# A Mamba-style mixer's clipped states: corrections on stretches of 256 steps with a lead of 32, in place of rows of 1024

## The reference

```python
def step(h, x_t):
    h = jnp.clip(h * A[None] + x_t[:, :, None] * Bm[None], -10.0, 10.0)
    y = jnp.einsum('bid,id->bi', h, C)
    return (h, y)
...
A = -jnp.clip(jnp.exp(A_log), -10.0, -0.01)
out_f = _ssm_scan(x_ssm, A, B_mat, C_mat, reverse=False)
out_b = _ssm_scan(x_ssm, A, B_mat, C_mat, reverse=True)
out = (out_f + out_b) * 0.5 * jax.nn.silu(gate)
return jnp.einsum('bli,di->bld', out, out_proj_w)
```

## Time and profile before

| | us |
|---|---|
| median of 3 runs | 3723.31 |
| lowest, highest | 3721.92, 3731.75 |
| the profiled execution's own time | 3721.55 |
| its span | 3719.6 |

### The profile page before, as it was taken

The page is one execution under the profiler, slowest core; times in us unless marked ns, Lnnn a source line. Parts: engine busy times, 40 slices in busy tenths (PEclk is TensorE's granted clock), DMA queues, the critical chain, the costliest instruction groups (busy, mean ns, idle before and its releaser), DMA issues. The chain is left out here.

```text
span 3719.6 us, 31897 instructions
## 1 busy us (share of the span) xinstructions
PE 2784.2 (75%) x10138; PEld 1394.3 (37%) x10146; DVE 2052.8 (55%) x3662; ACT 1359.4 (37%) x1980; POOL 897.8 (24%) x608
## 2 busy tenths in 40 slices
PE   2006898999999889999777867937888888287317
PEld 1003444555555534444344442423222222055303
DVE  7997432222222465655544476126766666587687
ACT  1003433111111256666434311415666666243003
POOL 0003565000000000000122402133777777200004
PEclk6558999999999999999778879979999999599558
DMA  2001121000000275455100020120000000100001
GB/s 50 0 0 46 46 62 47 0 0 0 0 0 0 49 139 146 138 147 139 32 1 1 1 71 20 57 58 30 1 1 2 7 1 0 31 1 1 2 0 29
DMA packets 107447, 125.99 MB, mean 34 GB/s; under 512 B 22283, under 2 KB 60300, under 8 KB 107052
## 3 DMA queue, kind: packets, MB, share of 16 engines
q1 hardware_dynamic: 105260, 120.13, 12.4%
q0 software_dynamic: 2048, 4.20, 0.4%
HBM read 108.55 MB, written 14.16 MB: 33 GB/s over the span
## 5 line engine op out<-in xcount | busy, mean ns | idle before, releaser
L2349 PE MATMUL dots_x<-all_xt,delta_wE 128*128 128x512 f32 x768 | 369.0, 614 | 70.1 <-DVE dots_g L2465 68.6
L2332 POOL TENSOR_TENSOR dots_pr<-dots_g 128x1536 f32<-128x1536 f32 (+2 forms) x98 | 296.1, 3043 | 143.6 <-DVE dots_g L2465 119.1
L1012 DVE SCALAR_TENSOR_TENSOR attn_sim<-attn_sc,attn_mask 128x512 f32<-128x512 f32 (+3 forms) x256 | 125.8, 491 | 316.9 <-PE attn_sc L938 313.8
L938 PE MATMUL attn_sc<-attn_q,attn_xb 128*128 128x512 f32 (+3 forms) x768 | 295.0, 486 | 0.0
L949 PE MATMUL attn_op<-attn_sim,attn_v 128*128 128x512 f32 (+3 forms) x768 | 295.0, 486 | 0.0
L2462 DVE TENSOR_TENSOR dots_m<-dots_x,dots_sg 128x512 f32<-128x512 f32 x256 | 170.3, 685 | 213.0 <-ACT dots_sg L2384 124.7
L1298 DVE TENSOR_TENSOR grp_h<-grp_sq,grp_cb 128x512 f32<-128x512 f32 x256 | 176.5, 692 | 192.1 <-ACT grp_sq L1186 171.8
L1126 PE MATMUL grp_po<-grp_h,grp_down 128*128 128x512 f32 x512 | 266.4, 602 | 6.0 <-DVE grp_h L1298 6.0
L1118 PE MATMUL grp_ph<-all_xt,grp_up 128*128 128x512 f32 x512 | 263.9, 598 | 0.5 <-ACT grp_sg L1202 0.5
L2349 PEld LDWEIGHTS dots_x<-all_xt,delta_wE 128*128 128x128 f32 x768 | 134.6, 190 | 304.6 <-issue 160.8
L1180 ACT ACTIVATE grp_r<-grp_ph 128x512 f32<-128x512 f32 x272 | 162.4, 597 | 185.5 <-PE grp_ph L1118 183.8
(11 more groups left out here) (614 smaller groups left out, 4961.9 us busy)
## 6 DMA issues: line engine op xcount, KB each, us to landing
grp_cb<-grp_combine SPq DMA_DIRECT2D x512, 128.0 KB, 3.2
mix_cb<-top_weights SPq DMA_DIRECT2D x64, 256.0 KB, 3.2
cap_xs<-cap_zero SPq DMA_DIRECT2D x7, 320.0 KB, 4.4
experts_xe<-cap_xs SPq DMA_DIRECT2D x7, 320.0 KB, 3.4
all_x<-in_L_attn_x_dram SPq DMA_DIRECT2D x4, 512.0 KB, 5.2
cap_w<-in_L_ffn_W_dram SPq DMA_DIRECT2D x1, 2048.0 KB
cap_ys<-experts_yo SPq DMA_DIRECT2D x8, 256.0 KB, 2.3
delta_h<-all_xn SPq DMA_DIRECT2D x1, 2048.0 KB
```

The lines of the kernel that those rows point to most:

```text
L938: nc.tensor.matmul(sc[k % SC][:, 0:w], xb[:, m * P:(m + 1) * P], q[:, par, n0:n0 + w], start=True, stop=True).then_inc(s_mm, 1)
L2332: nc.gpsimd.tensor_tensor(slot[w % SLOTS][:, at:at + n], a_, b_, ALU.mult).then_inc(pool_ready, 1)
L2349: nc.tensor.matmul(bank(n, sh)[:], wE[:, 1 - k % 2, a, sh], XTj[:, k // 2, par::2], start=True, stop=True).then_inc(u_mm, 1)
```

## The change

`LEAD, CHUNK` = 32, 256. Each row of 1024 steps is cut into `NCHUNK` = 4 stretches; a row and a stretch make a cell, 16 per batch (`NCELL`). The scan of S still covers the whole row. S now has 32 zero columns ahead of each row, so that each stretch can be read with the 32 steps before it.

- `reaches` keeps one largest value per stretch; `reach` grows from 64 to 256 columns, and with it what POOL reduces, the flags and the masks (16).
- `corrections` walks over 4 rows and in each over 4 stretches, and tests the mask of each cell.
- `correct` works on a window of 288 steps: the scan starts at zero, 32 steps before the stretch, and only the last 256 go into G.
- The semaphore `fix` becomes one per batch and counts 3 per state in place of 4, because the first `tensor_scalar` signals nothing any more.
- `d0`, `d1` and `q` shrink to the window, and the incoming weights are put in `y` instead of `q`.

The cut diff:

```diff
+    LEAD, CHUNK = 32, 256
+    NCHUNK = SEQ // CHUNK
+    NCELL = NSEG * NCHUNK
+    WINDOW, ROW = LEAD + CHUNK, LEAD + SEQ
...
-        d0 = s.sb("d0", [P, SEQ, 2])
+        d0 = s.sb("d0", [P, WINDOW, 2])
...
-        reach = s.sb("reach", [P, NSEG, DS])
+        reach = s.sb("reach", [P, NSEG, NCHUNK, DS])
...
-                def correct(b, k, d):
-
+                def correct(b, k, c_, d):
                     n = k * DS + d
-                    done = (b * (NSEG * DS) + n) * 4
-                    sk = S[:, bass.ds(k, 1), :].rearrange("p a t -> p (a t)")
-                    gk = G[:, bass.ds(k, 1), :].rearrange("p a t -> p (a t)")
+                    done = ((k * NCHUNK + c_) * DS + d) * 3
+                    sk = S_flat[:, bass.ds(k * ROW + c_ * CHUNK, WINDOW)]
+                    gk = G_flat[:, bass.ds((k * NCHUNK + c_) * CHUNK, CHUNK)]
...
-                    ts(d1[:, :, 0], sk, -1.0, L, ALU.mult, ALU.add).then_inc(fix, 1)
-                    ts(d1[:, :, 1], sk, L, None, ALU.add).then_inc(fix, 1)
-                    dve.wait_ge(fix, done + 2)
+                    ts(d1[:, :, 0], sk, -1.0, L, ALU.mult, ALU.add)
+                    ts(d1[:, :, 1], sk, L, None, ALU.add).then_inc(fix[b], 1)
+                    dve.wait_ge(fix[b], done + 1)
...
-                    stt(gk, q[:, :, 1], w, gk, ALU.mult, ALU.add).then_inc(fix, 1)
+                    stt(gk, q[:, LEAD:, 1], w, gk, ALU.mult, ALU.add).then_inc(fix[b], 1)
...
-                    c.link(redu(mx[:], S[:], AX.X, ALU.max, apply_absolute_value=True))
+                    c.link(redu(mx[:], S[:, :, LEAD:].rearrange("p k (c t) -> p k c t", t=CHUNK), AX.X, ALU.max, apply_absolute_value=True))
...
                     with dve.Fori(0, NSEG) as k:
-                        mask = dve.value_load(masks[0:1, bass.ds(k, 1)], min_val=0, max_val=2 ** DS - 1)
...
+                        with dve.Fori(0, NCHUNK) as c_:
+                            mask = dve.value_load(masks[0:1, bass.ds(k * NCHUNK + c_, 1)], min_val=0, max_val=2 ** DS - 1)
+                            for quad in range(DS // QUAD):
+                                with dve.If((mask & (((1 << QUAD) - 1) << (quad * QUAD))) > 0):
+                                    for d in range(quad * QUAD, (quad + 1) * QUAD):
+                                        with dve.If((mask & (1 << d)) > 0):
+                                            correct(b, k, c_, d)
+                                        with dve.Else():
+                                            dve.sem_inc(fix[b], 3)
+
+                                    dve.sem_inc(apart, 1)
+                                with dve.Else():
+                                    dve.sem_inc(fix[b], 3 * QUAD)
```

More of the change, by code:

```diff
@@ L266, in mixer_and_top2 @@
         limS, nCBS = (s.sb(n, [P, NSEG, DS]) for n in ("limS", "nCBS"))
-        d0 = s.sb("d0", [P, SEQ, 2])
[L268 to L271, removed]
-        xs, gate, y = (s.sb(n, [P, CT, SEQ]) for n in ("xs", "gate", "y"))
-        S, G = (s.sb(n, [P, NSEG, SEQ]) for n in ("S", "G"))
-        mx = s.sb("mx", [P, NSEG, 1])
-        reach = s.sb("reach", [P, NSEG, DS])
[L276 to L280, removed]
+        d0 = s.sb("d0", [P, WINDOW, 2])
+        d1 = s.sb("d1", [P, WINDOW, 2])
+        q = s.sb("q", [P, WINDOW, 2])
+        xs, gate, y = (s.sb(n, [P, CT, SEQ]) for n in ("xs", "gate", "y"))
+        wi = y[:, 0, 0:2 * CT * C].rearrange("p (k c) -> p k c", k=2 * CT)
+        wo = y[:, 1, 0:DI]
+        S = s.sb("S", [P, NSEG, ROW])
+        G = s.sb("G", [P, NSEG, SEQ])
+        S_flat, G_flat = S[:].rearrange("p k t -> p (k t)"), G[:].rearrange("p k t -> p (k t)")
+        mx = s.sb("mx", [P, NSEG, NCHUNK])
+        reach = s.sb("reach", [P, NSEG, NCHUNK, DS])
+        most = s.sb("most", [P, NCELL * DS])
+        bit = s.sb("bit", [1, NCELL, DS])
+        flags = s.sb("flags", [1, NCELL, DS])
+        mask_f = s.sb("mask_f", [1, NCELL])
+        masks = s.sb("masks", [1, NCELL], mybir.dt.int32)
         gw = s.sb("gw", [P, E])
@@ L304, in mixer_and_top2 @@
             "w_in", "c_in", "w_mm", "w_copied", "exp_ready", "pj_mm", "pj_used", "scanned", "y_ready"))
-        reach_ready, most_ready, out_mm, x_added, ch, fix, apart = (s.sem(n) for n in (
-            "reach_ready", "most_ready", "out_mm", "x_added", "vector_chain", "fix", "apart"))
+        reach_ready, most_ready, out_mm, x_added, ch, apart = (s.sem(n) for n in (
+            "reach_ready", "most_ready", "out_mm", "x_added", "vector_chain", "apart"))
+        fix = [s.sem(f"fix{b}") for b in range(BATCH)]
         gates_in, w1_in, w2_in, stats_done, var_ready, std_ready, xn_ready = (s.sem(n) for n in (
@@ L635, in largest @@
                     pool.sem_inc(apart, 1)
-                    nc.gpsimd.partition_all_reduce(most[:], reach[:].rearrange("p s d -> p (s d)"), P, bass.bass_isa.ReduceOp.max).then_inc(most_ready, 1)
+                    nc.gpsimd.partition_all_reduce(most[:], reach[:].rearrange("p s c d -> p (s c d)"), P, bass.bass_isa.ReduceOp.max).then_inc(most_ready, 1)
                 largest(0)
@@ L719, in corrections @@
                     with dve.Fori(0, NSEG) as k:
-                        mask = dve.value_load(masks[0:1, bass.ds(k, 1)], min_val=0, max_val=2 ** DS - 1)
[L721 to L731, removed]
+                        with dve.Fori(0, NCHUNK) as c_:
[10 more added lines that the diff above has]
+                                    dve.sem_inc(fix[b], 3 * QUAD)
                 def gated(b):
                     dve.wait_ge(pj_used, 8 * b + 8)
-                    dve.wait_ge(fix, (b + 1) * NSEG * DS * 4)
+                    dve.wait_ge(fix[b], NCELL * DS * 3)
                     for ct in range(CT):
@@ L788, in _ @@
                 c.link(ts(decay[:], al[:, 0, 0:1], -1.0, None, ALU.mult))
[L789 removed]
+                c.link(ts(d0[:, :, 0], al[:, 0, 0:1].to_broadcast([P, WINDOW]), 1.0, None, ALU.mult))
                 c.link(nc.vector.memset(d0[:, :, 1], -1.0))
+                c.link(nc.vector.memset(S[:, :, 0:LEAD], 0.0))
                 c.link(stt(nCB[:], Cm[:], -0.5, B[:], ALU.mult, ALU.mult))
```

11 lines of the change are left out of this document (6 added, 5 removed).

## The result

| | before | after |
|---|---|---|
| median, us | 3730.12 | 3716.92 |
| lowest, highest | 3721.92, 3734.82 | 3714.71, 3726.22 |
| runs | 12 | 12 |
| ratio, 95% interval | | 0.9972 (0.9962 to 0.9982) |
| the profiled execution's own time, span | 3721.55, 3719.6 | 3726.22, 3724.2 |

By the ratio the change saves 0.28%, some 10 us (7 to 14); the two medians alone differ by 13.2. In another set of runs (e5, nine of them) the ratio was 0.9977 (0.9968 to 0.9987). The forecast of 3704 was a gain of 19 us, a ratio of 0.995, which lies outside the interval. So the sign is right and about half of the gain is missing; by the bound of 0.3% used in the prediction, the change falls just within "no change".

What follows compares the result with a forecast made beforehand. It took PE's wait for the first gated product, set by batch 0's walk on DVE, as the bound: -79.9 + 54.6 + 5.4 + 0.8 = -19.1 us, 3702.4 for the profiled execution, stated as 3704; range 3687 to 3723.

Steps and rivals of the forecast that it cites:

- Part 2: DVE's walk: an empty cell costs 2.63 us, twelve more per batch 31.6, loop 1.5; batch 0 saves 79.9 in all.
- Part 3: Batches 1 to 3: the same 12 added cells make PE wait 31.5, 9.3 and 13.8 us for y, sum 54.6.
- the low clock: PE's clock drops during each new wait, so the small matmuls after it run slower: 1.8 us each, 5.4 together.
- Part 1: Batch 0 on DVE: 28 shorter corrections of 2.13 us each, 59.6 together, plus sequencer gaps of 42.3 us.
- The give-back: Batches 1 to 3: with POOL idle, slow y instructions take 1.22 in place of 2.18 us, returning 1.9, 2.8 and 2.8.
- The small terms: Reach products and flags on the path 0.8 us, wider flags and masks 0.4 per batch, the POOL reduction 0 (0 to 19).
- Each pass stalls: Rival: the walk's loop body misses the instruction buffer every pass, 1.8 us extra per cell, 115 on top, 3819; chance 0.07.
- Dear reduction: Rival: POOL's reduction over 256 columns costs 8 us in batch 0, up to 5.5 in batches 2 and 3; chance 0.12.
- Hidden walk: Rival: the added walk in batches 1 to 3 is hidden, giving 3704 - 60 = 3644 us; chance 0.03.
- More cells hit: Rival: more cells need corrections than worked out; four more with 28 corrections would cost 102 us; chance 0.02.
- wrong if: Signs against the forecast: mask loads over 2.9 apart, DVE waiting for POOL before flags, or no PE wait in batches 2 and 3.
- The first rival: Each pass stalls: all 64 cells count once cover is used up; beyond 0.3 us extra per cell the kernel is slower; chance 0.07.

Runs made afterwards that it cites:

- e5: The changed kernel measured once more, unaltered, as a comparison: 3739.8 us, ratio 0.9977 to the kernel before.
- e6: The changed kernel with its walk as one flat loop over 16 cells, one counter in place of two nested loops: 3732.8 us, ratio 0.9957 to the kernel before.
- e7: The changed kernel with stretches of 128 in place of 256, so 32 cells per batch: 3906.7 us, ratio 1.0418 to the kernel before.
- e1: The changed kernel with one test per row that skips rows without a set bit: 3683.8 us, ratio 0.9816 to the kernel before.
- e4: The kernel before, plus one test per batch that skips the walk where no row has a bit: 3756.5 against 3753 us, ratio 1.0007.
- e9: The changed kernel testing only one cell per row, where this input's hits lie: 3625.2 us, ratio 0.9722 to the kernel before.

## Why the prediction was half right

The bound was read rightly: PE waits for the first y, and the walk of batch 0 is its price. The mechanism came as described: 28 corrections, idle time called "issue" before every one of them, three new waits at the output product, of about 31, 9 and 14 us forecast and 31.45, 12.25 and 17.16 measured. The sum was forecast as -19.1 us for the stage and came out as -5.5:

| from, to | forecast | measured |
|---|---|---|
| start to output product 0 | -79.1 | -74.3 |
| product 0 to 1 | +31.5 | +33.0 |
| product 1 to 2 | +9.3 + 1.8 | +13.7 |
| product 2 to 3 | +13.8 + 1.8 | +19.7 |
| product 3 to the end | +1.8 | +2.4 |

(Measured: the starts in the earlier trace rows and in the profile after, for example 282.93 - 193.10 - (324.24 - 267.39) = 33.0.)

- **The step that failed is Part 2, the price of an empty cell**, which Part 3 multiplies. It was taken from rows of the old loop (2.63 us, plus 1.5 per batch for the loop). The new loop pays 116 ns more for the address ahead of the load and 22 more behind it, some 0.15 us a cell, on all 16 cells of a batch, not on the 12 new ones only, and 0.31 at each new row. Against the old walk, from the first to the last mask load, batch 1's is 42.24 - 8.08 = 34.2 us longer and those of batches 2 and 3 are 35.2 longer, where 33.1 was taken: 1.1 + 2.1 + 2.1 = 5.3 of the 13.6 missing. In batch 0 the twelve empty cells and the row steps took 34.5, 1.4 more. Together 6.7 us; the rest of the 13.6 is corrections and gaps in batch 0 (3.1), the low clock (1.5) and 2.3 of small pieces that I can't assign one by one. The diff showed the address, `k * NCHUNK + c_` in the mask's load; the list of built steps did not, since it has one ISA step ahead of the load before and after. I priced a dearer address in the corrections (0.1 each) and not in the cells. e6 undid the second counter and the stage fell by 12.9 us, to 18.6 below the kernel before. Of the 12.9, shorter walks are 11.1 (1.8 to the first y, then 3.1, 3.2 and 3.0 from first to last mask load, all against e5). That it ends so near the forecast is partly luck: in e6 the terms of the table are -76.3, +29.3, +11.4, +15.2 and +1.8, so that 2.8 too little in batch 0 stands against 2.2 too much forecast for batch 1.
- **Part 1 was right to 3 us of 105.** A correction took 2.21 us for 2.13 forecast (the tensor_scalars 0.28 and 0.40 to the next start for 0.25 and 0.37, the product 0.17 behind the scan), 2.2 us over 28. The scan took exactly the 1.36 worked out. The gaps come to 66.8 - 2.2 of idle, plus 27 times 0.49 of product, less 34.5 of empty cells, which is 43.2 for 42.3. The whole walk, from 45.52 (the end of the cast before it) to 188.04, was 142.5 for 137.9, and the first gated product came at 188.04, not near 182.
- **The cost of the low clock was a term of its own size, not 1.8 each.** The 32 products after a new wait took 5.17, 6.74 and 6.17 us where they had taken 3.73 to 3.75: 6.9 us for 5.4. Three stretches of the changed kernel (the last 9.5 us of the wait in batch 1, the output products of batch 1, those of batch 2) show the clock, the last but two of the numbers: 0.50, its lower level (1.2 of 2.4 GHz), while PE waits, 0.73 over the products that follow and 0.55 over those of batch 2:

```profile
273.40:282.90 9.50, 0.00 (x0) 0.00 (x0) 4.90 (x4) 0.00 (x0) 0.00 (x0) 0.50 0.00 1
282.90:288.10 5.20, 5.17 (x33) 5.17 (x34) 4.58 (x2) 0.00 (x0) 0.00 (x0) 0.73 0.00 0
385.40:392.20 6.80, 6.75 (x33) 6.75 (x34) 4.58 (x2) 0.00 (x0) 0.00 (x0) 0.55 0.00 0
```

- **What was hidden, and what came back.** The give-back was right: with POOL idle all four instructions of y took 1.22 or 1.23 us in each of batches 1 to 3. The small terms were not quite: 0.4 us more for flags and masks was 0.4, the reduction 0.5 more, and the walk of batch 0 began 1.0 us later for up to 0.8 forecast.
- **The rivals.** Each pass stalls: refuted. Behind the first cell of a walk, cells of one row lay 2.72 to 2.87 us apart with 16 cells and with 32 (e7; once 3.07), and the stall of 2 us came once per walk at most, in batches 2 and 3 and not in batch 1. (The "13 later passes" that the prediction counts against this rival are 7 in its rows.) The Trainium skill (Runtime: NRT & Kernel Launch, section on instruction fetch mechanics) ties a stall to a branch target outside the two blocks held. By that rule a body that did not fit would stall in every pass, and none did behind the first cell. That the stall is a fetch, no run here shows, nor why batch 1 has none. Dear reduction: refuted for this size, 1.06 to 1.23 us. Hidden walk: refuted by e1. More cells hit: no, the scans are 28.
- **The chances.** The "wrong if" bound on mask loads, over 2.9 us apart, was nearly reached (2.81, 2.89 and 2.88 on average in batches 1, 2 and 3). The first rival said that every extra microsecond per cell costs 64, and I did not apply this to the forecast's own 2.63. An uncertainty of 0.2 us a cell is 13 us, as much as the whole forecast's spread to one side, and with it "within 0.3%" would have had far more than 0.13.

The stage's 5.5 us and the 9 to 10 us measured for the whole program do not agree to the last microseconds. The profiled execution is one of twelve with a spread of 11.5 us. The traces show how much the later stages, whose code is the same, move by themselves: they took 3100.7 us in the profile before and 3110.8 after. Over half of these 10.1 us lies in one stretch of a later layer, from the first row of its `out_` tiles to the first row of the `sink_` tiles behind it: 258.9 us before and 265.2 after. It took 266.8 in e4, which is the kernel before with one test, and 258.9 in e9, which is the changed one with fewer cells, so it does not follow the change. The stage with the `attn_` tiles took 653 us in some profiled executions of either kernel and 656 in others. So the span of one execution says little about a difference of 10 us, and why the whole program gained more than the stage stays open.

## What to carry to other kernels

When a change cuts work into more pieces, price the piece that does nothing first: its cost times all pieces of all passes, not only the new ones, and ask for each whether its cover is used up. Price a sequencer's loop by the instructions of the new loop, address arithmetic included; here a second loop counter cost 12.9 us of the stage, over twice what the change left as a gain in it. And test from the outside in, batch, then cell, then bit: with that, one counter and a lead of 8, the same change was worth 96 us instead of 10.

## What the runs showed that was not expected

- A row address from one loop counter took 63 ns in DVE's sequencer, from two counters 179 (e5, e6); one load of a mask took 0.30 us in the median whatever the kernel, and a cell whose mask is zero still cost 1.50 (flat) to 1.63 us (two levels) with a single test.
- The reduction over the partitions on POOL took 0.54 us for 64 columns, 1.08 for 256 and 1.80 for 512 (medians): about 0.36 us plus 2.8 ns a column, far from in proportion.
- The scan on DVE took 825 ns at 320 columns, 1258 at 528, 1358 at 576, 2425 at 1088 and 4425 at 2048: 2.08 ns a column and 0.16 us on top.
- The 32 small products after a wait took 5.2 to 6.7 us with no order by the length of the wait (5.68 us after 138.8 us of waiting, 5.17 after 31.45, 6.74 after 12.25, 6.17 after 17.16). What decides when the clock comes back is open.
